# The skip-term copy of x in a gated recurrence: two of four chunks moved from one VectorE multiply to eight ScalarE activations

## The reference

```python
xh = xin.reshape(Bsz, L, H, P)                 # xin: a projection of the normed input
def step(carry, inp):
    Bx = jnp.einsum('bhp,bhn->bhpn', x_t, B_t)
    h = a_t[..., None, None] * h + g_t[..., None, None] * Bx + b_t[..., None, None] * prevBx
    y = jnp.einsum('bhpn,bhn->bhp', h, C_t)
    return ((h, Bx), y)
y = y + xh * D[None, None, :, None]            # the skip term
y = y * jax.nn.silu(z)
y = _rms(y, norm_w)
return y @ out_proj_w.T
```

## Time and profile before

| | |
|---|---|
| median of 3 runs | 1339.04 us (1335.22 to 1344.77) |
| the profiled execution | 1338.07 us |
| its span, first to last instruction | 1336.3 us |
| VectorE busy | 1224.1 us, 92% |
| TensorE matmuls busy | 1133.7 us, 85% |
| ScalarE busy | 797.7 us, 60% |
| GpSimd busy | 728.3 us, 55% |
| mean granted TensorE clock | 0.952 |

### The profile page before, as it was taken

The page is one execution under the profiler, slowest core; times in us unless marked ns, Lnnn a source line. Parts: engine busy times, 40 slices in busy tenths (PEclk is TensorE's granted clock), DMA queues, the critical chain, the costliest instruction groups (busy, mean ns, idle before and its releaser), DMA issues. The chain is left out here.

```text
span 1336.3 us, 30910 instructions
## 1 busy us (share of the span) xinstructions
PE 1133.7 (85%) x11514; PEld 832.9 (62%) x11514; DVE 1224.1 (92%) x1945; ACT 797.7 (60%) x1226; POOL 728.3 (55%) x562
## 2 busy tenths in 40 slices
PE   4873999989999999999999999899999999999810
PEld 3742666666666666666676666666766666667600
DVE  7774999989998999999998999899989999999688
ACT  5732666656666666666666666666666666666432
POOL 4001566656665566556664666566655665666523
PEclk9865999999999999999999999999999999999955
DMA  7535332343221422342223323342224323222033
GB/s 185 176 98 127 73 73 65 69 93 85 65 65 44 106 66 66 68 112 66 63 63 74 81 66 68 66 113 57 60 51 112 66 65 69 61 57 60 19 100 89
DMA packets 68513, 105.66 MB, mean 79 GB/s; under 512 B 14051, under 2 KB 32716, under 8 KB 68044
## 3 DMA queue, kind: packets, MB, share of 16 engines
q1 hardware_dynamic: 68364, 103.68, 33.2%
HBM read 24.73 MB, written 9.96 MB: 26 GB/s over the span
## 5 line engine op out<-in xcount | busy, mean ns | idle before, releaser
L1189 POOL TENSOR_TENSOR rot<-part 128x512 f32<-128x512 f32 x256 | 382.5, 1494 | 531.9 <-DVE part L1026 480.4
L1026 DVE SCALAR_TENSOR_TENSOR part<-bcs,k_prmT,trig 128x512 f32<-128x512 f32 x512 | 500.5, 1028 | 1.4 <-DMA trig<-tri 1.3
L1138 ACT ACTIVATE E<-d 128x512 f32<-128x512 f32 x256 | 151.7, 592 | 184.1 <-PE d L846 181.5
L864 PE MATMUL s<-rot 64*128 64x128 f32 x2048 | 149.7, 285 | 23.6 <-POOL rot L1189 19.1
L1044 DVE TENSOR_TENSOR M<-s,E 128x512 f32<-128x512 f32 x256 | 163.5, 678 | 2.4 <-PE s L864 1.8
L864 PEld LDWEIGHTS s<-rot 64*128 64x128 f32 x2048 | 126.9, 188 | 62.0 <-issue 54.6
L1198 POOL TENSOR_TENSOR ce<-rot,eb 128x512 f32<-128x512 f32 x128 | 160.1, 1272 | 3.0 <-ACT eb L1160 3.0
L1220 POOL TENSOR_TENSOR sqa<-sqa,sq 128x512 f32<-128x512 f32 x112 | 142.5, 1272 | 14.2 <-ACT sq L1143 6.2
L956 PE MATMUL y<-M,xk 128*64 128x128 f32 x2048 | 140.1, 279 | 0.0
L878 PEld LDWEIGHTS o<-k_w_o,yT 128*128 128x128 f32 x1024 | 132.5, 191 | 10.4 <-DVE yT L1103 5.0
L878 PE MATMUL o<-k_w_o,yT 128*128 128x128 f32 x1024 | 134.5, 275 | 2.6 <-DVE yT L1103 2.6
(11 more groups left out here) (234 smaller groups left out, 1792.8 us busy)
## 6 DMA issues: line engine op xcount, KB each, us to landing
trig<-tri SPq DMA_DIRECT2D x512, 128.0 KB, 2.4
bcs<-bc_t SPq DMA_DIRECT2D x16, 256.0 KB, 4.0
bcs<-bc_t SPq DMA_DIRECT2D x32, 128.0 KB, 3.9
a_big<-in_L_attn_u SPq DMA_DIRECT2D x4, 512.0 KB, 6.0
xn_t<-a_xnT SPq DMA_DIRECT2D x1, 2048.0 KB, 16.4
tc_t<-a_tcT SPq DMA_DIRECT2D x1, 2048.0 KB, 15.9
bc_t<-a_tmp SPq DMA_DIRECT2D x1, 2048.0 KB, 7.5
tcs<-tc_t SPq DMA_DIRECT2D x8, 256.0 KB, 3.0
```

Of the source, the lines that this page charges most:

```text
L864: last = nc.tensor.matmul(Sp[j][:, k], rot[rows, q % 2, p, 0, k], rot[rows, q % 2, p, 1, k], start=True, stop=True)
L1026: nc.vector.scalar_tensor_tensor(out=part[:, 2 * p + f, :], in0=bcs[:, (t + q // NQ) % 2, 2 * w + f, :], scalar=col, in1=trig[:, p, 1 - f, ...
L1138: nc.scalar.activation(E[:, h % 2, :], Dp[:], ACT.Exp).then_inc(e_ready, 1)
L1189: nc.gpsimd.tensor_tensor(rot[:, q % 2, p, w, :], part[:, 2 * p, :], part[:, 2 * p + 1, :], ALU.add).then_inc(rot_ready, 1)
```

## The change

Half 0 of `x_scaled` (chunks 0 and 1) writes `xk` only. Its `xc` is written by ScalarE instead, in a new function `skip_scaled`, with one activation (copy, times a scale read from memory) for each chunk and head: eight of 128x64. Half 1 is as before. In ScalarE's list `skip_scaled` for unit q + 1 stands behind the two `eb` and ahead of the two `sz`; it waits for `xk` of half 0 and for an old y. A new semaphore `xc_ready` tells TensorE, which waits for it ahead of the gate projection, as R[0] must have been read and `xc` been written.

```diff
@@ TensorE, before the first unit
             pe.wait_ge(rot_ready, at(T4, 0, 4))
+            pe.wait_ge(xc_ready, at(T1, 0, 1))
             for p in range(2):
@@ TensorE, ahead of the gate projection
                         if live(t, q + 1):
                             pe.wait_ge(xk_ready, at(T2, t, 2 * q + 2 + p + 1))
+                            pe.wait_ge(xc_ready, at(T1, t, q + 2))
@@ VectorE, x_scaled
-                for dst, f in ((xk, "kk"), (xc, "cc")):
+                for dst, f in ((xk, "kk"), (xc, "cc"))[0:1 + i]:
@@ ScalarE
+            def skip_scaled(t, q, tt):
+
+                act.wait_ge(xk_ready, at(T2, t, 2 * q + 1))
+                act.wait_ge(y_ready, at(T2, t, 2 * q - 2))
+                for c in range(2):
+                    for h in range(4):
+                        k = slice(64 * h, 64 * h + 64)
+                        at_head = tt * (CS * H) + c * H + 4 * (q % NQ) + h
+                        last = nc.scalar.activation(xc[:, q % 2, c, k], R[0][:, 256 * c + 64 * h:256 * c + 64 * h + 64], ACT.Copy,
+                                                    scale=K["cc"][:, at_head:at_head + 1])
+                last.then_inc(xc_ready, 1)
@@ ScalarE, before the first unit
             sines(0, 1)
+            skip_scaled(0, 0, 0)
             decays(0, 0, 0)
@@ ScalarE, in a unit, behind the two eb
                         nc.scalar.activation(eb[:, p, :], Dp[:], ACT.Exp).then_inc(ebs_ready, 1)
+                    if live(t, q + 1):
+                        skip_scaled(t, q + 1, t if q < NQ - 1 else t + 1)
                     for p in range(2):
```

More of the change, by code:

```diff
@@ L706, in units @@
         ebs_ready, ce_ready = sem("ebs_ready"), sem("ce_ready")
-        xk_ready, bw_ready = sem("xk_ready"), sem("bw_ready")
+        xk_ready, xc_ready, bw_ready = sem("xk_ready"), sem("xc_ready"), sem("bw_ready")
         sz_ready, yt_ready, sq_ready = sem("sz_ready"), sem("yt_ready"), sem("sq_ready")
@@ L1115, in _ @@
         def _(act):
-            for s in (rounded, sin_ready, absd, e_ready, ebs_ready, sz_ready, sq_ready, acc_done, ssq_taken):
+            for s in (rounded, sin_ready, absd, xc_ready, e_ready, ebs_ready, sz_ready, sq_ready, acc_done, ssq_taken):
                 act.sem_inc(s, 1)
```

## The result

The changed kernel takes 1342.81 us (median of 20 runs, 1340.08 to 1346.79) against 1338.86 us (20 runs) for the kernel before: a ratio of 1.003, 95% interval 1.0019 to 1.0041. That is 4 us slower (0.3%, beyond the noise), where the forecast said 14. The range of 1334 to 1374 us holds it; the predicted 1353 us does not fit. The profiled execution took 1341.73 us, its span is 1339.7 us.

What follows compares the result with a forecast made beforehand. The prediction took the mutual waits of VectorE and TensorE as the bound. Nothing gained by removal, plus 3.07 us per odd and 0.71 per even stage, four of each, 15.1 on 1338.07, gave 1353 us; range 1334 to 1374.

Steps and rivals of the forecast that it cites:

- The removal at nothing: VectorE's half-0 `xc` multiply, 0.60 us a unit: removing it only lengthens the wait for L830, so gains nothing.
- The rival with VectorE as the bound: VectorE's busy time counts: units up to 0.60 us shorter, 1300 us; chance 0.10.
- The term of 0.5 us a unit in an odd stage: Lateness left on TensorE's half of the loop of mutual waits, at q = 1, 3, 4, 5, 6: 0.5 us each.
- The lateness: TensorE's L950 and all behind it start 1.1 us late, waiting for ScalarE's `xc` (0.2 and 1.5 by the bounds).
- The price of the eight: ScalarE's eight 128x64 activations behind the second `eb`: 2.07 us, with bounds of 1.2 and 2.47.
- three slacks: Odd-stage slack ahead of L864 (0.17 us), the second `sqa` (0.35) and L830 (about 0.07), absorbing part of TensorE's delay.
- the ring: VectorE and TensorE wait for each other once a unit, by `bw` and L830; this decides time, not busy share.
- The way: TensorE's delay passes through ScalarE's `sq`, GpSimd's `sqa`, VectorE's `part` and `ang` to L830; chance 0.55.
- the sum of squares: L987 at q = 7 waits for the second `sqa`, late by about 0.57 us (odd stage) and 0.36 (even).
- The hidden rival: L825's wait takes the lateness: 0.15 us in about 20 odd units or nothing, 1338 to 1342 us; chance 0.27.
- The rival above the bounds: ScalarE's queue itself binds, activations over 0.30 us each and `M` waiting too: 1380 us and above; chance 0.08.

Runs made afterwards that it cites:

- the run with `rot` later: Kernel before, with GpSimd's third `rot` of a unit waiting until VectorE's last `part` is through: 1353.68 us, ratio 1.0102.
- with `ang` first: Changed kernel, with VectorE doing `ang` and the states before the next unit's first `part`: 1341.11 us, ratio 1.002.
- the run from SBUF: Changed kernel, but VectorE writes both `xc`, and ScalarE's eight activations read an SBUF constant and write a spare tile: 1354.73 us, ratio 1.0117.
- The run from PSUM bank D: Changed kernel, but VectorE writes both `xc`, and ScalarE's eight activations read PSUM bank D and write a spare tile: 1342.91 us, ratio 1.003.
- a second: Kernel before, with GpSimd's third `rot` delayed past the last `part` and also `ang` and the states ahead of the first `part`: 1325.71 us, ratio 0.9882.

## Why the prediction was right in kind and wrong in size

*The removal at nothing: right.* The wait for `xk` was to grow from 22 to about 60 us; it is 57.0, and 59.1 with the multiply simply left out. The run without that multiply shows it by itself (ratio 0.9996). The rival with VectorE as the bound wanted the second `xk` sooner than 7.58 us after `bw`; it starts at 7.73. (Of the 55 waits in the earlier trace rows one is ahead of a first `xk`, so ten units show none, not nine; five of these have 0.06 to 0.13 us of idle time there.)

*What failed.* The term of 0.5 us a unit in an odd stage was mis-sized: it measured 0.15, with a first `part` of 1.14 to 1.29 us where I wrote 1.5 or more, and a unit of 17.34 where I wrote 17.7. The term is what three slacks leave of the lateness. The lateness was taken too large, first of all by the price of the eight activations, and the slacks too small.

*The price of the eight: wrong, and the first step that failed.* I took 2.07 us, 0.25 for each after the first; they take 1.74, one every 0.20. I read L598's pace as 4.86 us by 16, as if the sixteen ran without a pause. Two more views of the kernel before, the timeline of half a us within them, and the lines of the window 47 to 53 us (busy us, mean ns of one, idle us just before them), show that they don't:

```profile
47.98 0.88 ACT L598 ACTIVATE k_w_o<-a_ps,k_prmT 128x128 f32<-128x128 f32 x3
...
L598 ACT ACTIVATE k_w_o<-a_ps,k_prmT 128x128 f32<-128x128 f32 x16 | 4.6, 368 | 0.4
```

They are busy for 4.6 of the 4.86 us; of the 0.4 us of idle time 0.1 stands ahead of the first, and the other 0.3 between groups of four. Three that do run back to back take 0.88 us, so one every (0.88 - 0.368) / 2 = 0.256 us; less 64 columns at the forecast's 0.7 to 0.8 ns, 0.05, that is 0.20: what was measured. With it the activations would have come to 7 x 0.20 + 0.32 = 1.72 us, and the lateness to 1.1 - 0.35 = 0.75. The Trainium skill, page "ScalarE: Activation LUTs", section "What ACT_TABLE_LOAD costs", gives 0.24 us for each by its own figures; this case agrees where the source is SBUF (2.01 us for eight) and not where it is PSUM (1.74).

*The lateness: 0.90, not 1.1.* It is larger than the price alone would make it, because the first two matmuls of the projection start 0.15 us after the last activation and, with those behind them, take 1.79 us to L952 (622.43 to 624.22) where I put 0.06, which I had read from no row, and 1.72.

*The slack: each step a little too small.* L864 is 0.65 late (it absorbs 0.24, I had 0.17). The second `E` is 0.60 late, `sq` 0.61, the `sqa` pair 0.22 (it ends 3.13 us after `bw` begins, 2.91 before): the slack ahead of the second addition was 0.39, I had 0.35 (I halved the pair; the second addition starts at 632.91, not 632.84). There is a second way to the same 0.22 that I did not see, by the first square. Four lines of before, and three of after, from windows that hold only one `sqa` of the pair:

```profile
629.62 0.60 ACT L1138 ACTIVATE E<-d 128x512 f32<-128x512 f32 x1 [1.28 <-PE d L846]
630.23 1.27 POOL L1189 TENSOR_TENSOR rot<-part 128x512 f32<-128x512 f32 x1 [0.63 <-DVE part L1026]
630.79 0.63 ACT L1143 ACTIVATE sq<-yT 128x512 f32<-128x512 f32 x1 [0.57 <-DVE yT L1103]
632.91 1.27 POOL L1220 TENSOR_TENSOR sqa<-sqa,sq 128x512 f32<-128x512 f32 x1
...
629.77 0.60 ACT L1140 ACTIVATE E<-d 128x512 f32<-128x512 f32 x1 [1.28 <-PE d L846]
630.96 1.27 POOL L1237 TENSOR_TENSOR sqa<-sqa,sq 128x512 f32<-128x512 f32 x1 [0.19 <-ACT sq L1157]
632.38 1.28 POOL L1237 TENSOR_TENSOR sqa<-sqa,sq 128x512 f32<-128x512 f32 x1
```

Before, the first addition (631.49) follows `rot` at once, its `sq` having waited for `yT`. After, the first `E`, 0.89 late, holds that `sq` back (630.26), and the first addition waits 0.19 us for it and is 0.21 late. The second stands 0.14 behind the end of the first in both kernels, and after the change also 0.08 behind its own `sq`, just as the first stands behind its `sq`. So each way by itself makes it as late as it is, and these two traces do not tell them apart (in the run with `rot` later it is the second square, for which the addition waits 0.40 us). `part` ends 0.54 us after the addition ends, as the forecast took it, and so does `ang` 0.21 late. L830 starts 0.06 us after `ang` ends, where I had kept 0.15 for signal and weights: it is 0.05 late, but now its weights load while it starts, not ahead, and it takes 1.13 instead of 1.03. Together 0.15 us on the ring, the 0.05 and the 0.10, where the forecast had 0.5. The three slacks in a row (0.24, 0.39, 0.16) take 0.79 where the forecast had 0.59, and the lateness is 0.90 where it had 1.1: 0.2 us from either side turn the remainder of 0.5 into 0.1, and that is the 10 us between 14 and 4.

*The way: right, and shown.* Without the addition the loss in the units goes; with `ang` ahead of `part` it goes; with the work of ScalarE alone it is all there; and at a lateness of 1.16 us `part` takes 1.52 us and a unit is 0.40 longer. That GpSimd's addition holds an operation of VectorE with two inputs in SBUF until it is through, the assumption of the forecast, is what `part` shows at 0.73 us alone, 1.14 and 1.52 in the larger doses, and 1.77 where the addition began just ahead of it. The Trainium skill, page "SBUF — State Buffer", section "SBUF: two separate sides", calls this an exclusive lock for the whole instruction; the 0.54 us from the addition's end to `part`'s end in both kernels agree.

*By place.* q = 2 costs nothing, as said (18.00 against 17.99). The last unit of an odd stage costs 0.42, where the forecast had 0.5 for q = 6 and 0.57 for the sum of squares; with `ang` first 0.22 is left (20.56), which is the sum of squares late with the second `sqa`. The last unit of an even stage costs 0.01 where I had 0.07 and 0.36: the slacks are larger than I took them, and the `sqa` pair ends 2.91 us after `bw` begins there in both kernels. At q = 0 of an odd stage I counted nothing and it costs 0.15.

*What I did not have:* the lower clock at the head of a stage, 1.0 us and 0.2 in the unit behind it. The new wait for `xc` meets a pause for `eb` that is there already (0.78 us at L853 in the kernel before too).

*The chances.* Within 1%, which came, had 0.42, and slower 0.48. The hidden rival was nearest in size: it named about 3 us for activations nearer to 0.14 than to 0.25 us, and 0.15 us a unit. That the unit's 0.15 is the measured one is luck: there it was what L825's wait could not take of 1.1 us, and it came by `part` and `ang`. The rival above the bounds did not come: `M` idles 2.5 us in all, 2.4 before. That `M` had some 0.2 us to spare I had read from no row.

*Open:* why the clock falls at one head of a stage and not at the other seven of the same profile, which have the same waits of 0.78 and 1.55 us. With 1.82 us in the run from SBUF it falls at three of eight, all of even stages. Not open is the stretch ahead of the units, 2 us shorter in the profile after: the profiles of the kernel before's variants reach the first unit's L825 at 132.0 to 139.9 us, so that it differs by that much from one execution to the next.

## What to carry to other kernels

Before moving work off the busiest engine, find the last thing that the next instruction on it waits for: 62 multiplies of 0.60 us on an engine busy for 92% were worth nothing, and the same multiply one place later some 18 us. Work that is moved costs where it lands, in front of whatever is queued behind it, and what is left of its lateness behind several slacks is a small difference of large numbers, so price it from instructions that truly run back to back (look for idle time within the group) and carry the error of the price through the sum. When an operation of one engine is held by another engine's, moving the other one away helps only if what then comes late does not collide in its turn: the one edit alone lost 15 us, with a second gained 13.

## What I had not expected of the hardware

A short activation with a scale from memory was faster from PSUM than from SBUF: eight of 128x64 in 1.74 against 2.01 us, at 0.338 us for the last of them. The run from PSUM bank D wrote the same spare bf16 tile as the run from SBUF and took 1.74 too, so the source alone makes the difference. And the granted clock fell from its higher to its lower level (0.54 over 3.3 us) where TensorE had waited 0.78 us and then 1.55 us with five matmuls between, though it had been at 0.99 over the 14 us before; seven like places in the same execution kept it.
